# The pairwise stage of a four-layer graph network: steps planned over pairs of query tiles, with sums of both halves at twelve of 29 steps

## The reference

```
# layer 1 of the reference, for each batch
q = feat @ W1.T                       # 2048 x 64
k = feat @ W2.T                       # 2048 x 64
e = relu(q[:, None, :, :] + k[:, :, None, :])
scores = einsum('bijd,d->bij', e, a)  # 2048 x 2048 scores, 64 channels each
att = softmax(scores + mask, axis=-1) # mask: -1e22 where adj <= 0
return att @ feat
```

## Time and profile before

| | us |
|---|---|
| median of 3 runs (lowest, highest) | 12219.96 (12218.97, 12223.52) |
| the profiled execution | 12227.2 |
| its span, first to last instruction | 12225.4 |
| PE busy | 11903.6 (97%) |
| DVE busy | 10279.6 (84%) |
| ACT busy | 9349.5 (76%) |
| the pairwise stage of one batch, first array to the last tile's minimum | 936.7 (3295.13 to 4231.85) |

### The profile page before, as it was taken

One profiled execution on the slowest core, in us unless ns is written; L12 is line 12 of the kernel. 1 busy time (PEld: TensorE's weight loads), 2 busy tenths in 40 slices (PEclk: granted clock), 3 DMA queues, 4 the chain that ended last, 5 costly groups with the idle time before them and its releaser, 6 DMA issues.

```text
span 12225.4 us, 264459 instructions
## 1 busy us (share of the span) xinstructions
PE 11903.6 (97%) x118401; PEld 5910.8 (48%) x118401; DVE 10279.6 (84%) x12373; ACT 9349.5 (76%) x7633; POOL 459.0 (4%) x636
## 2 busy tenths in 40 slices
PE   7999999999999999999999999999999999999999
PEld 3333853338433384333843348433484334843348
DVE  4999849998599975999759997599975999759997
ACT  3998739987499874988748987489874898749986
POOL 1000000000000000000000000000000000000000
PEclk9999999999999999999999999999999999999999
DMA  2000320003200031000310003100031000410013
GB/s 75 19 22 22 107 79 22 19 22 115 74 19 19 26 120 66 19 19 27 130 55 19 19 28 136 48 19 19 31 139 42 19 22 31 141 37 19 22 32 106
DMA packets 206183, 611.30 MB, mean 50 GB/s; under 512 B 45440, under 2 KB 137216, under 8 KB 139520
## 3 DMA queue, kind: packets, MB, share of 16 engines
q1 hardware_dynamic: 184176, 450.72, 10.8%
q0 software_dynamic: 20880, 143.66, 3.2%
HBM read 556.47 MB, written 8.39 MB: 46 GB/s over the span
## 4 chain that ended last, share of the span: by engine, by line
DVE 53%; PE 44%; issue 1%; SPq 1%; ACT 0%; DMA 0%; POOL 0%; DVEq 0%
DVE E L881 34%; PE ps L1341 10%; DVE E L889 9%; PE ps L1361 8%; PE ps L1448 7%; PE ps L1461 4%; PE ps L1521 4%; PE ps L1428 4%; PE ps L1376 3%; DVE T L904 2%; PE ps L1507 2%; DVE E L879 1%; DVE HW L915 1%; DVE adj_ring L896 1%; SPq L415 1%
## 5 line engine op out<-in xcount | busy, mean ns | idle before, releaser
L611 ACT ACTIVATE E<-QB,KBP 128x2048 f32<-128x2048 f32 x3328 | 6398.6, 1994 | 705.6 <-PE ps L1361 691.0
L1361 PE MATMUL ps<-E,s_win 128*32 128x512 f32 x61440 | 6741.2, 594 | 115.3 <-DVE E L889 71.1
L881 DVE TENSOR_SCALAR E<-QA,KLO,KHI 128x2048 f32<-128x2048 f32 x4096 | 5252.2, 1339 | 21.1 <-DVE nmin L904 18.1
L1361 PEld LDWEIGHTS ps<-E,s_win 128*32 128x32 f32 x61440 | 1981.5, 110 | 4672.4 <-issue 4177.4
L1013 DVE CUSTOM_DVE_ANT_0 T<-ps,adj_ring 128x2048 f32<-128x2048 f32 x512 | 1171.8, 2289 | 75.3 <-PE ps L1428 72.0
L889 DVE SCALAR_TENSOR_TENSOR E<-QB,KBN,E 128x2048 f32<-128x2048 f32 x512 | 1200.2, 2344 | 0.0
L643 ACT ACTIVATE T<-T,nmin 128x2048 f32<-128x2048 f32 x512 | 1029.0, 2010 | 183.6 <-DVE nmin L1013 183.6
L1448 PE MATMUL ps<-ident,T 128*128 128x128 f32 x8192 | 1098.9, 276 | 16.9 <-DVE HT L975 12.0
L1448 PEld LDWEIGHTS ps<-ident,T 128*128 128x128 f32 x8192 | 913.5, 141 | 200.5 <-ACT PT L523 71.2
L523 ACT ACTIVATE AGG<-ps 128x512 f32<-128x512 f32 x224 | 126.8, 596 | 1012.5 <-PE ps L1341 980.9
L1341 PE MATMUL ps<-adj_res,H 128*128 128x512 f32 x2048 | 889.5, 592 | 0.0
(11 more groups left out here) (147 smaller groups left out, 7680.3 us busy)
## 6 DMA issues: line engine op xcount, KB each, us to landing
adj_ring<-in_adj SPq DMA_DIRECT2D x384, 1024.0 KB, 5.0
adj_res<-in_adj POOLq DMA_DIRECT2D x128, 1024.0 KB, 5.9
qcur<-AGG SPq DMA_DIRECT2D x896, 16.0 KB, 2.8
qcur<-HT SPq DMA_DIRECT2D x896, 16.0 KB, 2.2
HW<-in_x POOLq DMA_DIRECT2D x9, 1024.0 KB, 7.1
X<-in_x SPq DMA_DIRECT2D x128, 64.0 KB, 1.9
out_x<-X SPq DMA_DIRECT2D x8, 1024.0 KB, 16.7
wq_r<-in_L_gnn_Wq SPq DMA_DIRECT2D x4, 64.0 KB, 2.3
```

The lines of the kernel that those rows point to most:

```text
L611: last = nc.scalar.activation(E[:, e_slot(t, k) + g, :], QB[:, :], ACT.Relu, bias=KBP[:, col:col + 1])
L881: last = nc.vector.tensor_scalar(dst, QA[:, :], KLO[:, col:col + 1], KHI[:, col:col + 1], ALU.max, ALU.min)
L1361: last = mm(ps[QROWS * g:QROWS * (g + 1), 4 * u + c, :], win, E[:, s + g, c * CH:(c + 1) * CH], start=(k == 0), stop=(k == NS - 1), tile_p ...
```

## The change

The steps are now planned over two tiles together (`pair_plan`, 29 steps where there were 30). NS is `4 * SETS - 3` = 29 and MID is 15. Twelve steps of a pair hold a fused set (three in each column group), where a pair had eight before. Column groups 0 and 1 begin the second tile at step 15, groups 2 and 3 at step 14, so in step 14 the groups write into different halves of the PSUM. ScalarE now writes two arrays in 27 of the 29 steps and one in the other two. Where a step has no two second halves to write, it takes first halves: a Relu of QA with a scale pointer `s12` and a bias pointer KAP, which TensorE reads with the signs of `s1_win`. A line in `evac_k1` makes KAP.

E has 13 slots and HW is the fourteenth. Slots are handed out one by one in a ring of 14 (`e_slot`), and each array waits for the step that last used its slot (`slot_freed`): for the slots of groups 0 and 1 that is step n - 4, for groups 2 and 3 step n - 3.

T1 and PT1 are gone. `min1` writes the scores into the ring buffer that held the mask, and the exponential, the transposes, the copies and `out1` work there. `ring_free` is gone: SyncE loads a ring buffer once `out1` of the tile that used it is done, and VectorE no longer waits for the end of `min1`. In the tail `finish1` moves from step 11 to step 12 of a tile, the statistics from 12 to 13, and `evac_ht2` from step 14 to step 13 (in step numbers of its tile; the second tile of a pair has the steps 0 to 13).

The diff, cut to its core:

```diff
-EQ = 3
-FUSED = (4, 8, 6, 12)
-NS = 2 * SETS - 1
+SLOTS = 14
+NS = 4 * SETS - 3
+PAIRS = NT // 2
+MID = NS // 2 + 1
+FUSED = ((4, 18, 25), (10, 21, 27), (2, 8, 14), (6, 12, 23))
+SCALAR_ONE = (5, 19)
...
+def pair_plan():
...
+        left = 1 if i in SCALAR_ONE else 2
+        order = sorted(range(4), key=lambda g: ("second", "first", "fused").index(row[g][1]))
+        by_act = [g for g in order if row[g][1] != "fused"][:left]
...
+def e_slot(p, i, g):
+    return (4 * (p * NS + i) + g) % SLOTS
+def slot_freed(p, i, g):
+    return (4 * (p * NS + i) + g - SLOTS) // 4 + 1
...
+            return HW[:, :] if i == SLOTS - 1 else E[:, i, :]
...
 # SyncE
-                    else:
-                        sp.wait_ge(ring_free, b * NT + k + 1)
+                    elif k >= 2:
+                        sp.wait_ge(o1_ps, b * NT + k - 1)
...
 # ScalarE, step1
+                        if kind == "second":
+                            last = nc.scalar.activation(dst, QB[:, :], ACT.Relu, bias=KBP[:, col:col + 1])
+                        else:
+                            last = nc.scalar.activation(dst, QA[:, :], ACT.Relu, bias=KAP[:, col:col + 1], scale=s12[:, 0:1])
...
+            def pair1(b, p):
+                keys(b, 2 * p)
+                for i in range(NS):
+                    step1(b, p, i)
+                    u, k = i // MID, i % MID
+                    t = 2 * p + u
...
-                    if t in (5, 9, 13) and k == 14:
+                    if t in (5, 9, 13) and k == 13:
                         evac_ht2(b, t // 4 - 1, 1)
...
 # VectorE
+                nc.vector.tensor_scalar(KAP[:, cols], of_a, ns12[:, :], None, ALU.mult)
...
 # min1
-                dve.wait_ge(e_used, (T + 1) * NS)
+                dve.wait_ge(e_used, tile_ends(T))
...
-                    out=T1[:, :], in0=ps[:, 4 * u:4 * u + 4, :].rearrange("p c n -> p (c n)"), in1=ring[:, u, :],
+                    out=ring[:, u, :], in0=ps[:, 4 * u:4 * u + 4, :].rearrange("p c n -> p (c n)"), in1=ring[:, u, :],
...
-                dve.wait_ge(t1_rdy, T + 1)
-                dve.sem_inc(ring_free, 1)
...
-                    if tail and k == 11:
+                    if tail and k == 12:
                         finish1(t - 1, T - 1, 1 - u)
...
 # TensorE, step1
+                        signed = s1_win if by_act and kind == "first" else s_win
...
+                                  start=i in (0, second_begins(g)), stop=i in (second_begins(g) - 1, NS - 1),
```

More of the change, by code:

```diff
@@ L53, with second_begins, tile_ends @@
 STEPS = NT * HEADS
-EQ = 3
-FUSED = (4, 8, 6, 12)
-NS = 2 * SETS - 1
-SCALAR_TWO = tuple(k for k in range(NS) if k != 1)
-def column_group(g):
-    kinds, m = [], 0
-    while len(kinds) < NS:
-        if len(kinds) == FUSED[g]:
-            kinds.append(("fused", m))
-        else:
-            kinds += [("first", m), ("second", m)] if g < 2 else [("second", m), ("first", m)]
-        m += 1
-    return kinds
-def tile_plan():
-    plan = []
-    for row in zip(*[column_group(g) for g in range(4)]):
-        left = 2 if len(plan) in SCALAR_TWO else 1
-        step = []
-        for kind, m in row:
-            by_act = kind == "second" and left > 0
-            left -= by_act
-            step.append((kind, m, by_act))
-        plan.append(step)
-    return plan
-PLAN = tile_plan()
-def e_slot(t, k):
-    return 4 * ((t * NS + k) % EQ)
+SLOTS = 14
[3 more added lines that the diff above has]
+FUSED = ((4, 18, 25), (10, 21, 27), (2, 8, 14), (6, 12, 23))
+FUSED_STEPS = sorted(i for steps in FUSED for i in steps)
+SCALAR_ONE = (5, 19)
+def second_begins(g):
+    return MID if g < 2 else MID - 1
+def column_group(g):
+    slots = []
+    for tile, over in enumerate((range(second_begins(g)), range(second_begins(g), NS))):
+        m, half = 0, None
+        for i in over:
+            if half is not None and i not in FUSED[g]:
+                slots.append((tile, "second", half))
+                half = None
+                continue
+            if i in FUSED[g]:
+                slots.append((tile, "fused", m))
+            else:
+                slots.append((tile, "first", m))
+                half = m
+            m += 1
+    return slots
+def pair_plan():
+    plan = []
+    for i, row in enumerate(zip(*[column_group(g) for g in range(4)])):
+        left = 1 if i in SCALAR_ONE else 2
+        order = sorted(range(4), key=lambda g: ("second", "first", "fused").index(row[g][1]))
+        by_act = [g for g in order if row[g][1] != "fused"][:left]
+        plan.append([(tile, kind, m, g in by_act) for g, (tile, kind, m) in enumerate(row)])
+    return plan
+PLAN = pair_plan()
+def tile_ends(T):
+    return T // 2 * NS + (MID if T % 2 == 0 else NS)
+def e_slot(p, i, g):
+    return (4 * (p * NS + i) + g) % SLOTS
+def slot_freed(p, i, g):
+    return (4 * (p * NS + i) + g - SLOTS) // 4 + 1
 def k_col(t, g, m):
@@ L260, in build @@
             KBP = sb("KBP", [P, N // GR], where=ph)
+            KAP = sb("KAP", [P, N // GR], where=ph)
         with ExitStack() as ph:
@@ L615, in exp1 @@
                 act.wait_ge(t1_rdy, T + 1)
-                nc.scalar.activation(T1[:, :], T1[:, :], ACT.Exp, bias=nmin1[:, u:u + 1], scale=-1.0,
+                nc.scalar.activation(ring[:, u, :], ring[:, u, :], ACT.Exp, bias=nmin1[:, u:u + 1], scale=-1.0,
                                      accum_out=rsum1[:, u:u + 1]).then_inc(p1_rdy, 1)
@@ L621, in evac1 @@
                     act.wait_ge(pt1_ps, T * NC + g + 1)
-                    last = evac(PT1[:, g * CH:(g + 1) * CH], ps[:, 4 * u + g, :])
+                    last = evac(ring[:, u, g * CH:(g + 1) * CH], ps[:, 4 * u + g, :])
                 last.then_inc(pt1_act, 1)
-            def tile1(b, t, u, tail):
-                T = b * NT + t
-                keys(b, t)
-                for k in range(NS):
-                    step1(b, t, k)
+            def pair1(b, p):
[4 more added lines that the diff above has]
+                    t = 2 * p + u
+                    T, tail = b * NT + t, t > 0
                     if tail and k == 3:
@@ L1214, in _ @@
                 dve.wait_ge(qb_sb, (b + 1) * NC)
-                for t in range(NT):
-                    tile1(b, t, t % 2, t > 0)
+                for p in range(PAIRS):
+                    pair1(b, p)
                 T = b * NT + NT - 1
@@ L1375, in out1, with pair1 @@
                         rows = slice(QROWS * g, QROWS * (g + 1))
-                        last = mm(ps[rows, 4 * u, 0:D], PT1[:, j * P + QROWS * g:j * P + QROWS * (g + 1)], H[:, j, :],
+                        last = mm(ps[rows, 4 * u, 0:D], ring[:, u, j * P + QROWS * g:j * P + QROWS * (g + 1)], H[:, j, :],
                                   start=(j == 0), stop=(j == NT - 1), tile_position=(0, QROWS * g))
                 last.then_inc(o1_ps, 1)
-            def tile1(b, t, u, tail):
-                T = b * NT + t
-                for k in range(NS):
-                    step1(b, t, k, u)
+            def pair1(b, p):
+                for i in range(NS):
+                    step1(b, p, i)
+                    u, k = i // MID, i % MID
+                    t = 2 * p + u
+                    T, tail = b * NT + t, t > 0
                     if tail and k == 5:
```

112 lines of the change are left out of this document (57 added, 55 removed).

## The result

The changed kernel takes 12138.47 us (median of 4 runs, 12128.08 to 12144.21), the kernel before 12221.74 on the same chips: ratio 0.9928, 95% interval 0.9916 to 0.994. That is 83 us less. The profiled execution, the shortest of the four, has a span of 12126.3 us against 12225.4, 99 us less. The prediction was 12080 us, within 12000 to 12185: the direction came true, the waits stand where they were expected, and the gain came out at six tenths of its size.

A forecast was written before the change was run, and what follows sets the result against it. VectorE's own work, plus one wait for TensorE's product, was taken to set the period. 3.2 us a pair gave -205; copies +58, KAP +3 and edges +3 made -141, so 12080 us, range 12000 to 12185.

The forecast's parts named there:

- VectorE's, TensorE's and ScalarE's totals: Work of each engine in a pair of tiles after the change: 112.4, 110.5 and 113.1 us.
- Meeting 1: VectorE's wait for TensorE's product ahead of the addition to X goes, giving 2 x 1.04 us a pair.
- Meeting 2: VectorE's minimum at step 1 waits 0.7 us for TensorE's last step, once a pair; VectorE's period becomes 113.1 us.
- the sum: All terms added: -205 for 64 pairs, +58 copies, +3 KAP, +3 edges, giving -141 us.
- Meeting 3: Waits for free slots: the latest for VectorE, step 13's, has about 1 us in hand, so nothing was taken.
- Meeting 4: ScalarE's copy of the features' transposes waits 3.8 us; VectorE loses 2.4 us in each of 24 pairs, +58 us.
- From the profiled execution to the median: The median of the runs was put 7 us below the profiled execution: 12086 becomes 12079 us.
- ScalarE's pointer: The second pointer, the scale, in 13 of ScalarE's first halves a pair costs 0.09 us each, 1.2 us in all.
- Rival C: ScalarE's spare time kept things smooth; six meetings a pair cost 0.5 us each, nothing gained: 12210 us, 10%.
- Rivals A: Only engine totals count and the features' copies cost nothing: -205 us, 12015 us; chance 17%.
- B: TensorE is the bound and the step is worth its whole time: -371 us, 11850 us; chance 3%.
- D: ScalarE becomes the bound through its two-pointer first halves; at 0.4 us above the plain 1.894: 12335 us; chance 7%.

The follow-up runs named there:

- experiment 5: The changed kernel with the addition to X put back from step 12 to step 11 of a tile: 12207.62 us.
- experiment 6: The kernel before with only the addition to X moved from step 11 to 12 and the statistics from 12 to 13: 12195.65 us.
- experiment 3: The changed kernel with 12 slots in E and none in HW, instead of 14: 12133.86 us.
- Experiment 1: The changed kernel with TensorE's transposes of the next layer's features after step 11 of tiles 5, 9 and 13, not step 12: 12061.63 us.
- experiment 10: The kernel of Experiment 1 with VectorE's minimum after step 2 instead of step 1: 12073.54 us.
- experiment 7: The kernel of experiment 6 without VectorE's wait for its minimum's end; SyncE waits for the minimum instead of `ring_free`: 12169.66 us.
- experiment 9: The kernel of Experiment 1 with 30 steps and 8 sums, and the minimum after step 2 instead of step 1: 12085.74 us.

## Why the prediction was right, and where its size was off

*VectorE's, TensorE's and ScalarE's totals:* right. 112.4, 110.5 and 113.1 were predicted; the plain pair has 112.55, 111.49 and 113.16 busy. TensorE's is 1.0 more, though its steps kept their 3.44 (13.87 for four, with the latency of the last).

*Meeting 1, the product:* the wait went as predicted (L954 has none), and experiment 5 brought it back. Its value was reckoned wrongly as 2 x 1.04 a pair. In the kernel before, alone, it gave 28 of 133 us, since most of it came back in the same loop, 0.60 of 1.04 as a wait for a slot (experiment 6). In the changed plan it is worth 0.83 in a plain pair (experiment 5).

*Meeting 2, the minimum:* right in kind, 0.95 and not 0.7. The term took the path from the sum of step 23, which is not the one that ends last. In the trace the chain of waits leaves VectorE earlier (start, length, what):

```profile
3461.70 1.21 DVE HW L912
...
3462.95 7.07 PE ps L1394 x64
3470.03 1.90 PE ps L1303 x16
3471.92 13.91 PE ps L1394 x128
3485.83 3.49 PE ps L1410 x128
...
3503.30 2.29 DVE adj_ring L936
```

From 3462.95, behind the array of step 19, TensorE runs ten steps, the transposes and the product, 40.1 us, and then the minimum starts at 3503.30. The pair takes 113.58 instead of 113.1: 0.48 x 64 = 31 us of the 42 that the profiled execution lies above the sum.

*Meeting 3, slots:* nothing was taken, and 12 slots for 14 cost nothing (experiment 3). But ScalarE does wait for the slot of step 10, 0.41 us in the changed kernel, so that its period is 113.16 + 0.41 as well, level with 113.58. The prediction had looked at VectorE's slots alone.

*Meeting 4, the features' copy:* right in place and in the way it is handed on. ScalarE waited 3.10 (3.8 predicted), the minimum got 0.7 more (0.5), the copies 1.61 (1.9). The cost of one was 2.4 by prediction; the two pairs take 115.30 + 116.35 - 2 x 113.58 - 1.44 = 3.05 more, with the 1.44 of normalising from the kernel before. Experiment 1 parts it: 2.80 is the late copy, against 1.9 predicted, and the rest is in the pair with the transposes, which moving them does not shorten. The mis-sized term is the first: only what VectorE lost up to its copies was counted. ScalarE stays 3 us late to the pair's end, having nothing to make it up with, and VectorE loses the rest at the next minima (0.43 at 3680.70 and 1.13 at 3734.95). 0.65 x 24 = 16 us. With the 31 above that is 47 against 42.

*From the profiled execution to the median:* the sum took 7 us off, because the median before lay below the profiled run. After the change it lies 10 above it (12138.47 and 12128.08). These 17 us are the spread of the runs; with the 42 they make up the distance from the sum's 12079 to 12138.

*ScalarE's pointer:* 0.09 us, as taken from the row of the first pointer, and as the Trainium skill has it ("ScalarE: Activation LUTs", section "What ACT_TABLE_LOAD costs": about 93 ns for each pointer operand; 2097 - 2006 = 91 here).

*Rival C* (the lost spare time of ScalarE): the argument against it, that ScalarE has 8 us in hand at the minimum, left out the slots. ScalarE and TensorE do close a loop there, 0.41 us a pair in the changed kernel and 2.04 in one pattern of experiment 10. Its price of 3 us in every pair did not come. *Rivals A, B and D* are out: the copies counted, TensorE was not the bound, and the first halves cost 2.10.

In all, added in this order: 28 us by moving the addition to X, 26 by the minimum's wait, 108 by the plan with ScalarE's first halves and slots (experiment 7 to 1), and 77 given back by the features' copy. The sum had the two effects of the tail at 133 + 29 and gave the plan a small part; in this order it is the other way round. The parts depend on the order: in the changed plan the addition to X is worth 69 (experiment 5), and 84 of the 108 come with 30 steps too, once the minimum stands a step later (experiment 7 to 9). That the pair came within 0.5 us of the 113.1 is in part luck: VectorE's, TensorE's and ScalarE's paths end there nearly level, and the values that the sum gave to the single moves were not the ones measured.

## What to carry to other kernels

Where two or three engines are each 97% full, the period is not the largest total: it is the longest path through the meetings, and this can run half a tile on one engine and half on the other. Find it in the chain of waits by the points at which it changes engines, and move the instruction that closes the loop (here a minimum one step later was worth 137 us in one plan, and nothing or less in another) before taking work away. And when an order is planned more tightly, go through every small instruction that borrowed another engine's spare time: a copy one step nearer to its source cost nearly as much as all that was gained.

## What the runs showed of the hardware

On ScalarE a scale taken from a pointer costs 90 ns on top of the bias pointer (2097 against 2007 ns at 2048 elements). On VectorE a wait for the 128x2048 minimum just ahead and a count of VectorE's own behind that wait cost 0.23 us together (2.45 against 2.22 from start to start), 0.12 of it the wait (2.34).
